# TensorE's attention steps gathered between feed-forward runs in a fused decoder layer

## The chip, the cores and the metric

The kernel runs on one core of one Trainium2 chip. The metric is the device time of one execution in microseconds (us), as the median of several; lower is better.

## The reference, cut to what matters

One decoder layer over x of 32 sequences, 128 tokens each, width 256, all float32:

```
x = x + linear_attention(layernorm(x))          # 16 heads of 16, phi = elu + 1, causal running sums, q/k/v/o projections
x = x + cross_attention(layernorm(x), ctx)      # 16 heads of 16, softmax(q k / 4) v, no output projection
x = x + ffn(layernorm(x))                       # ternary weights with one scale per output:
      h = silu(s1 * (x w1)) * (s2 * (x w2))     # 256 -> 1024, "gate"
      h = gelu(h1s * (h h1)); h = gelu(h2s * (h h2))   # 1024 -> 1024 twice, "hidden"
      y = w3s * (h w3)                          # 1024 -> 256, "w3"
```

## The kernel before, in words

**Tiles.** The 32 sequences are worked through in 16 groups g of two sequences (256 tokens) for the two attentions, and in 8 turns f of four sequences (512 tokens) for the feed-forward. Turn f takes groups 2f and 2f+1, and runs while the attention of later groups runs beside it. Products that need float32 accuracy are made of parts: a value is split in a rounded and a rest part, and the matmuls of the parts are summed in PSUM.

**Steps and due times.** The order of every engine's work is written out by a planner at build time. Each step (a name, a group or turn, and an index n) is put with `put` on one or more engines, with a due time in nominal us: for attention `begin(g) + stretch * t`, for the feed-forward `FF0 + TURN * f + t`. Sorted by due time, these lists are the program of each engine: SyncE (`sync`) issues the DMAs, GpSimd (`gpsimd`), ScalarE (`scalar`), VectorE (`vector`) and TensorE (`tensor`) compute. Engines run their list in order, and wait at each step on semaphores. The due times only sort; they are not enforced, and in the trace most steps run some 15 to 30 us later than their nominal time.

**TensorE's steps.** The feed-forward steps are `gate`, `hidden` and `w3`, of four matmuls of 512 columns each (lines 982, 997, 1012). The attention steps are projections (`q`, `k`, `xk`, `xq`, line 825; `v`, `xv`, line 835; `project`, line 937: 12 or 6 matmuls of 256 columns), transposes (`ln1T`, `ln2T`, `x2T`, `xn3T`, line 814; `lin_turn`, `x_turn`, line 860; `o_turn`, line 928; `shift`, line 955), and the "quarter" steps, which use the array by quarters: scores (`lin_scores`, `max`, `x_scores`, lines 871 and 878) and sums (`lin_sums`, `x_sums`, line 851). After sorting, a loop over TensorE's list moves quarter steps: where two of them have only feed-forward steps between them and their due times differ by less than JOIN (1.44), the earlier is moved behind those feed-forward steps, to stand next to the later.

**Banks.** After that a second pass gives each TensorE step the PSUM banks that come free first by the due times of the steps that read them. A step waits, before it writes a bank, for the reader of the bank's last content. So `max` n=1 of a group, which needs four banks, waits for four readers (for example VectorE's `q` of the next group, or `max_of`).

**The other engines' steps named below.** On VectorE: `gated` (lines 776, 779) multiplies gates, `max_of` (line 745) takes maxima out of the `max` banks, `q` (lines 653, 658) forms phi(q), `lin_turn` (lines 666 to 673) divides, `lin_mask` (line 728) masks, `o_turn` (line 647) makes a rest part, `ln1_stats` (lines 637 to 640) and `ln1` (line 643) belong to the first layernorm, and `low_bits` (lines 794, 796) checks a piece of the weights, 48 times in all, each piece loaded before by SyncE's `load_bits` (line 432) into one buffer. `load_bits` waits until the `low_bits` before it is done. SyncE's `ring` (line 423) loads a weight chunk into one of four slots when TensorE has used up the slot's last content.

Of the kernel before, what the change touches and what calls it, by code (L numbers as in the profile page):

```python
# [5 lines left out]
def decoder_layer_program(nc, x, ctxT, wqT, wkT, wvT, woT, bv, bo, xqT, xkT, xvT,  # L6
# [37 lines left out]
    def put(start, step, g, n=0, stretch=1.0, **slots):  # L44
        for engine, t in slots.items():
            engines[engine].append((start + stretch * t, step, g, n))

    for g in range(G):
        at, stretch = begin(g)
        early = g < len(EARLY)  # L50

        def steady(step, n=0, **slots):
            put(at, step, g, n, stretch, **slots)

        steady("load_x", sync=-26.63)
# [6 lines left out]
        steady("v", tensor=-3.78, vector=-0.18)
        steady("load_xb", sync=1.22)
        steady("bias", gpsimd=9.03)
        steady("load_ctx", sync=-1.48)
        steady("ctx", scalar=9.15, gpsimd=8.15)
        for b in range(GB):
            steady("lin_scores", b, tensor=-0.89 + 4.6 * b)
        for n in range(NU):
            u = 0.34 + 1.09 * n  # L70
            steady("lin_mask", n, vector=u + 0.02)
        for b in range(GB):
            for h in range(2):
                if early:
                    u = 2.15 + 5.15 * b + 2.64 * h
                else:
                    u = 4.18 + 7.14 * b + 0.02 * h
                steady("lin_sums", 2 * b + h, tensor=u - 0.32)
            steady("lin_out", b, scalar=u + 1.21)
            u = 7.2 + 4.71 * b  # L80
            steady("lin_turn", b, tensor=u - 0.39, vector=u + 0.5)
            steady("o_turn", b, tensor=u + 0.93, scalar=u + 3.59, vector=u + 2.25)
            steady("project", b, tensor=u + 3.88, vector=u + 5.03, gpsimd=u + 6.25)
            steady("ln2", b, vector=u + 6.35)
        steady("ln2T", tensor=17.76, scalar=17.95, vector=18.63)
        steady("xq", tensor=21.95, scalar=22.34)
        steady("xk", tensor=16.76, scalar=20.6)
        steady("xv", tensor=11.7, scalar=16.21)
        for b in range(GB):
            steady("max", b, tensor=23.23 + 2 * b)  # L90
            steady("x_scores", b, tensor=29.28 + 3 * b)
        for n in range(NU):
            b, u = n // 4, n % 4
            steady("max_of", n, vector=24.37 + .72 * n)
            w = 30.6 + 3.45 * b + 0.09 * u
            steady("x_exp", n, scalar=w + 0.1)
        for b in range(GB):
            for h in range(2):
                if early:
                    u = 31.71 + 3.3 * b + 0.45 * h  # L100
                else:
                    u = 31.3 + 3.72 * b + 0.01 * h
# [22 lines left out]
    def out_of_window(t):  # L125

        for first, last in stretches:
            if first < t < last:
                return last
        return t  # L130

    for f in range(NF):
        at = FF0 + TURN * f
        for p in range(2):
            put(at, "xn3T", 2 * f + p, tensor=-10.49 + 2.6 * p, scalar=-5.65 + 2.6 * p, vector=-5.32 + 2.6 * p)
            put(at, "x2T", 2 * f + p, tensor=11 + 1.5 * p, scalar=12.78 + 1.5 * p)
        put(at, "keep_xn", f, sync=16.34)
        put(at, "keep_x2", f, sync=14.37)
        for m in range(KH):
            u = 2 * QUARTER * m  # L140
            for z in range(2):
                put(at, "gate", f, 2 * m + z, tensor=u + QUARTER * z)
            put(at, "tanh", f, m, scalar=u + QUARTER + 0.93)
            put(at, "gated", f, m, vector=u + 2 * QUARTER + 0.64)
            put(at, "gate_round", f, m, scalar=u + 2 * QUARTER + 4.43)
            put(at, "gate_rest", f, m, gpsimd=u + 2 * QUARTER + 5.72)
        for n in range(2 * KH):
            for q in range(4):
                k = 4 * n + q
                if n % KH < 2:  # L150
                    k = 8 * (n // 2) + (6 + n % 2 if q == 3 else 3 * (n % 2) + q)
                put(at, "hidden", f, 4 * n + q, tensor=QUARTER * (2 * KH + k))
            u = QUARTER * (2 * KH + 4 * (n + 1) + (n % KH == 0) * 3) + .5
            put(at, "gelu", f, n, scalar=out_of_window(at + u) - at)
            put(at, "gelu_rest", f, n, vector=out_of_window(at + u) - at + 1.6)
        for c in range(C):
            for q in range(4):
                k = 6 + c if q == 3 else 3 * c + q
                put(at, "w3", f, 4 * c + q, tensor=QUARTER * (10 * KH + k))
            put(at, "out", f, c, vector=TURN + .4 + c, sync=TURN + 1.6 + c)  # L160
        for j in range(NCH):
            if f == 0 and j < RING:
                u = -44.53 + j
            elif j < RING:
                u = (-7.74, -1, -6, 1.8)[j]
# [46 lines left out]
    with outer:  # L212
# [7 lines left out]
        ctx = ExitStack()  # L220
        with ctx:
            def sb(name, shape, dt=F32):
                return ctx.enter_context(nc.sbuf_tensor(name, shape, dt))
# [26 lines left out]
            v, xv = sb("v", [P, GB, H, 2 * HD]), sb("xv", [P, GB, H, 2 * HD])  # L250
# [19 lines left out]
            ring = sb("weight_ring", [P, RING, KH * P], F32R)  # L270
# [72 lines left out]
            while pending:  # L343
                t, step, g, n = pending.pop()
# [681 lines left out]
        ctx = ExitStack()  # L1026
        with ctx:
# [7 lines left out]
            gate = sb("general_gate", [P, FT])  # L1035
# [233 lines left out]
```

How the kernel before makes its waits and increments, by code:

```python
            def wait_freed(eng, step, g, n):  # L367
                _, s, count = release(step, g, n)
                eng.wait_ge(s, count)
# [8 lines left out]
            def wait_count(eng, s, count):  # L378
                if count > 0:
                    eng.wait_ge(s, count)
# [5 lines left out]
            def wait_full(eng, f, tile):  # L387
                f, tile = (f, tile - NFULL) if tile >= NFULL else (f - 1, tile - NFULL + 3 * KH)
                if f >= 0:
                    if tile < KH:
                        eng.wait_ge(gate_lo, KH * f + tile + 1)
                    else:
                        eng.wait_ge(h_lo, 2 * KH * f + tile - KH + 1)
# [14 lines left out]
                def load_ring(f, j):  # L408
                    if j >= RING:
                        used = j - RING
                        if used < 4:
                            eng.wait_ge(gate_psum, 2 * KH * f + 4 * used + 4)
                        else:
                            eng.wait_ge(h_psum, 2 * KH * f + used - 3)
                    elif f > 0:
                        if j % 2 == 0:
                            eng.wait_ge(w3_half, C * (f - 1) + j // 2 + 1)
                        else:
                            eng.wait_ge(o_psum, C * (f - 1) + j // 2 + 1)
                    if f == 0:
                        eng.wait_ge(w_copied[j // RING % 2], 16 * RING * (j // RING // 2 + 1))
                    n = WSRC[j].shape[1]
                    eng.dma_start(ring[:, j % RING, 0:n].bitcast(F32), w_d[j, :, 0:n]).then_inc(ring_loaded[j % RING], 16)
```

## Time and profile before

| | us |
|---|---|
| three runs: median (lowest, highest) | 1128.82 (1127.39, 1129.23) |
| the profiled execution: its own time | 1130.69 |
| its span | 1128.9 |
| TensorE matmul busy | 1087.5 |
| VectorE busy | 694.1 |
| ScalarE busy | 541.8 |
| GpSimd busy | 196.0 |

The profile is of one execution. Busy times are sums over an engine's instructions. PE is TensorE (its records of consecutive matmuls overlap, so distances are read here from start to start), DVE is VectorE, ACT is ScalarE, POOL is GpSimd, SPq is SyncE's DMA queue.

### The profile page before, as it was taken

What the parts mean: (1) busy time and instruction counts of PE and PEld (TensorE: products, weight loads), DVE (VectorE), ACT (ScalarE), POOL (GpSimd) and SP (SyncE); (2) the same over time, 40 slices, a digit from 0 to 9 for tenths busy, and PEclk for the clock granted to TensorE, in tenths of its full rate; (3) what the DMA queues carried; (4) which work ended last, traced back from release to release, by engine and by line L of the source; (5) the groups of instructions that cost most, each with busy time, mean ns of one, the idle gap of its engine ahead of it and who ended that gap; (6) DMA issues with size and microseconds to landing.
All of it is one profiled execution on the core that took longest, in us unless ns stands there. A gap on an engine that the chain in (4) does not pass through costs nothing.

```text
span 1128.9 us, 25213 instructions
## 1 busy us (share of the span) xinstructions
PE 1087.5 (96%) x10114; PEld 900.6 (80%) x10114; DVE 694.1 (61%) x1580; ACT 541.8 (48%) x909; POOL 196.0 (17%) x266
## 2 busy tenths in 40 slices
PE   4878999999999999999999999999999999999997
PEld 4767878888888888888888888888788888878886
DVE  5678764558656676567656686466765667534521
ACT  3244644536446454645546364373544645354532
POOL 1122320013201132022210222002320023100300
PEclk8899999999999999999999999999999999999999
DMA  3243554344323444324533354233433344434742
GB/s 117 66 163 110 185 186 144 122 138 162 129 92 114 135 160 131 104 85 145 188 113 104 99 172 137 94 123 126 163 104 109 110 150 141 132 108 131 242 154 76
DMA packets 62502, 148.62 MB, mean 132 GB/s; under 512 B 5936, under 2 KB 21424, under 8 KB 62384
## 3 DMA queue, kind: packets, MB, share of 16 engines
q1 hardware_dynamic: 58928, 135.44, 36.6%
q10 hardware_dynamic: 3456, 11.54, 3.2%
q8 instruction: 83, 1.36, 0.5%
q14 instruction: 35, 0.29, 0.1%
HBM read 130.17 MB, written 28.31 MB: 140 GB/s over the span
## 4 chain that ended last, share of the span: by engine, by line
PE 93%; DVE 3%; issue 1%; ACT 1%; DMA 1%; ACTq 0%; POOL 0%; SPq 0%; DVEq 0%; POOLq 0%
PE bank L997 42%; PE bank L982 10%; PE bank L878 9%; PE bank L825 8%; PE bank L851 5%; PE bank L1012 5%; PE bank L835 4%; PE bank L860 3%; PE bank L814 2%; PE bank L937 2%; PE bank L871 1%; PE bank L928 1%; PE bank L955 1%; DVE att_l L728 0%; DMA weight_ring<-weights_scratch 0%
## 5 line engine op out<-in xcount | busy, mean ns | idle before, releaser
L997 PE MATMUL bank<-hidden_b,weight_ring 128*128 128x512 f32 x1024 | 257.5, 398 | 0.3
L997 PE MATMUL bank<-hidden_a,weight_ring 128*128 128x512 f32 x1024 | 256.1, 397 | 0.0
L997 PEld LDWEIGHTS bank<-hidden_a,weight_ring 128*128 128x128 f32 x1024 | 185.7, 188 | 38.8 <-issue 3.4
L997 PEld LDWEIGHTS bank<-hidden_b,weight_ring 128*128 128x128 f32 x1024 | 184.9, 188 | 39.6 <-issue 3.8
L625 ACT ACTIVATE hidden_full<-bank,columns_sb 128x512 f32<-128x512 f32 x128 | 88.2, 689 | 232.9 <-PE bank L997 232.7
L982 PE MATMUL bank<-hidden_b,weight_ring 128*128 128x512 f32 x512 | 132.3, 399 | 0.5 <-DVE ex L658 0.3
L511 POOL TENSOR_TENSOR hidden_a<-hidden_full,hidden_a 128x512 fp32r<-128x512 f32 x64 | 82.3, 1289 | 194.0 <-ACT hidden_a L620 194.0
L728 DVE TENSOR_TENSOR att_l<-bank,cst 128x512 f32<-128x512 f32 x128 | 85.5, 684 | 39.7 <-PE bank L878 34.9
L982 PEld LDWEIGHTS bank<-hidden_b,weight_ring 128*128 128x128 f32 x512 | 92.2, 189 | 18.2 <-DMA weight_ring<-weights_scratch 0.7
L485 POOL TENSOR_TENSOR ve<-mv,eps 128x1 f32<-128x1 f32 (+1 forms) x80 | 19.7, 247 | 487.7 <-DVE mv L640 487.7
L784 DVE TENSOR_TENSOR hidden_a<-hidden_full,hidden_a 128x512 fp32r<-128x512 f32 x64 | 44.2, 691 | 79.0 <-ACT hidden_a L631 78.9
L745 DVE TENSOR_REDUCE mx<-bank 128x4 f32<-128x512 f32 x128 | 82.6, 682 | 9.2 <-PE bank L878 9.1
L784 DVE TENSOR_TENSOR hidden_b<-hidden_full,hidden_b 128x512 fp32r<-128x512 f32 x64 | 43.9, 686 | 67.4 <-ACT hidden_b L631 67.3
L595 ACT ACTIVATE att_x<-bank 128x512 f32<-128x512 f32 x128 | 66.1, 603 | 37.7 <-PE bank L878 37.6
L1012 PE MATMUL bank<-hidden_a,weight_ring 128*128 128x512 f32 x256 | 67.0, 399 | 0.0
L530 ACT ACTIVATE sums<-bank 128x512 f32<-128x512 f32 x64 | 38.5, 602 | 52.5 <-PE bank L851 52.5
L615 ACT ACTIVATE hidden_full<-bank,s1h 128x512 f32<-128x512 f32 x64 | 44.0, 688 | 35.8 <-PE bank L982 35.4
L776 DVE SCALAR_TENSOR_TENSOR hidden_full<-hidden_full,bank 128x512 f32<-128x512 f32 x64 | 43.7, 683 | 28.3 <-ACT hidden_full L615 28.1
L1012 PEld LDWEIGHTS bank<-hidden_a,weight_ring 128*128 128x128 f32 x256 | 45.8, 188 | 8.0
L500 POOL TENSOR_TENSOR ctxs<-ctx_in,ctxs 128x512 fp32r<-128x512 f32 x16 | 21.0, 1313 | 175.9 <-ACT ctxs L545 175.9
L488 POOL TENSOR_TENSOR rstd<-ve,mhalf 128x1 f32<-128x1 f32 (+1 forms) x80 | 50.0, 625 | 6.3
L779 DVE SCALAR_TENSOR_TENSOR hidden_full<-bank,s,hidden_full 128x512 f32<-128x512 f32 x64 | 48.1, 751 | 4.5 <-PE bank L982 2.4
(119 smaller groups left out, 1659.8 us busy)
## 6 DMA issues: line engine op xcount, KB each, us to landing
weight_ring<-weights_scratch SPq DMA_DIRECT2D x160, 512.0 KB, 3.4
weights_scratch<-in_h ACTq DMA_DIRECT2D x16, 512.0 KB, 4.7
xn3T_scratch<-hidden_b SPq DMA_DIRECT2D x16, 512.0 KB, 6.0
weight_ring<-weights_scratch SPq DMA_DIRECT2D x32, 256.0 KB, 2.7
weight_bits<-in_h SPq DMA_DIRECT2D x32, 256.0 KB, 3.8
x_in<-in_x SPq DMA_DIRECT2D x16, 256.0 KB, 3.6
xb<-in_x SPq DMA_DIRECT2D x16, 256.0 KB, 4.5
ctx_in<-in_ctxT SPq DMA_DIRECT2D x16, 256.0 KB, 4.3
```

The lines of the kernel that those rows point to most:

```text
L511: eng.tensor_tensor(HA[:, 1, n, :], full[:, n % NFULL, :], HA[:, 0, n, :].bitcast(F32), ALU.subtract)\
L595: eng.activation(att_x[:, (NU * g + n) % NX, :, :], pbank("x_scores", g, n)[:, :].rearrange("p (j s) -> p j s", j=4), ACT.Exp, scale=SCALE ...
L625: eng.activation(full[:, (KH + n) % NFULL, :], pbank("hidden", g, n)[:, :], ACT.Gelu, scale=sc).then_inc(h_full, 1)
L728: eng.tensor_tensor(att_l[:, (NU * g + n) % NL, :, :], pbank("lin_scores", g, n)[:, :].rearrange("p (j s) -> p j s", j=4), causal.rearrang ...
L745: eng.tensor_reduce(mx[:, b, 4 * r:4 * r + 4], pbank("max", g, n)[:, :].rearrange("p (j t) -> p j t", j=4), AX.X, ALU.max).then_inc(max_do ...
L784: eng.tensor_tensor(dst[:, 1, m, :], full[:, (KH + n) % NFULL, :], dst[:, 0, m, :].bitcast(F32), ALU.subtract)\
L825: mm = eng.matmul(pbank(step, g)[:, m * T:(m + 1) * T], w[:, i, c, m * P:(m + 1) * P], src[:, j, c, :], start=(c + i + j == 0), stop=(c == ...
L851: mm = eng.matmul(pbank(step, g, b)[32 * j:32 * j + 32, u * S:(u + 1) * S], vt[:, b, 8 * m + 2 * (n % 4) + e, :], att[:, (NU * g + n) % sl ...
L878: mm = eng.matmul(pbank(step, g, 4 * b + r)[:, j * S:(j + 1) * S], stationary(rows, e, m, b), moving(rows, e, m, b), start=not shifted, st ...
L982: mm = eng.matmul(pbank(step, g, n)[:, :], ring[:, n // 4, at_:at_ + P], HB[:, part, kk, :], start=(kk == 0 and part == 0), stop=(kk == C ...
L997: mm = eng.matmul(pbank(step, g, n)[:, :], ring[:, slot, kk * P:(kk + 1) * P], src[:, part, kk, :], start=(kk == 0 and part == 0), stop=(k ...
L1012: mm = eng.matmul(pbank(step, g, c)[:, :], ring[:, slot, kk % 4 * P:(kk % 4 + 1) * P], HA[:, part, kk, :], start=(kk == 0 and part == 0), ...
```

## The change

GATHER = 1 is new. The loop that moves TensorE's steps now looks at every step that is not feed-forward. Two such steps with only feed-forward steps between them are put side by side when their due times differ by less than JOIN (both quarter steps) or less than GATHER (all other pairs). With it most due times are written anew, of all engines. Nothing that is computed changes.

```diff
+    GATHER = 1
@@ attention, due times (a selection)
-        steady("load_x", sync=-26.63)
-        steady("ln1_stats", vector=-17.81, gpsimd=-16.41)
-        steady("ln1", vector=-13.07)
+        steady("load_x", sync=-25.57)
+        steady("ln1_stats", vector=-18.45, gpsimd=-15.85)
+        steady("ln1", vector=-11.62)
-        steady("q", tensor=-7.66, scalar=-6.73, vector=-5.37)
+        steady("q", tensor=-7.67, scalar=-6.7, vector=-5)
-            steady("lin_out", b, scalar=u + 1.21)
+            steady("lin_out", b, scalar=u + 1.36)
-        steady("xk", tensor=16.76, scalar=20.6)
-        steady("xv", tensor=11.7, scalar=16.21)
+        steady("xk", tensor=16, scalar=21.24)
+        steady("xv", tensor=12.01, scalar=15.67)
...
@@ feed-forward, SyncE and the weight check
-            put(at, "xn3T", 2 * f + p, tensor=-10.49 + 2.6 * p, scalar=-5.65 + 2.6 * p, vector=-5.32 + 2.6 * p)
+            put(at, "xn3T", 2 * f + p, tensor=-10.67 + 2.6 * p, scalar=-5.69 + 2.6 * p, vector=-5.46 + 2.6 * p)
-            put(at, "ring", f, j, sync=u - 4.82)
+            put(at, "ring", f, j, sync=u - 4.32)
-            u = 185.23 + 117.17 * i + 18.33 * j
-            put(0, "load_bits", i, j, sync=u - 4.56)
-            put(0, "low_bits", i, j, vector=u + 11.29)
+            u = 185.23 + 116.9 * i + 18.33 * j
+            put(0, "load_bits", i, j, sync=u - 12.42)
+            put(0, "low_bits", i, j, vector=u + 11.2)
...
@@ the loop over TensorE's list
     order = program["tensor"]
+    feed_forward = ("gate", "hidden", "w3")
+    quarters = ("lin_scores", "max", "x_scores", "lin_sums", "x_sums")
     for i in reversed(range(len(order))):
-        if order[i][1] in ("lin_scores", "max", "x_scores", "lin_sums", "x_sums"):
+        if order[i][1] not in feed_forward:
             j = i - 1
-            while j > 0 and order[j][1] in ("gate", "hidden", "w3"):
+            while j > 0 and order[j][1] in feed_forward:
                 j -= 1
-            if j >= 0 and order[j][1] in ("lin_scores", "max", "x_scores", "lin_sums", "x_sums") and order[i][0] - order[j][0] < JOIN:
+            both = order[i][1] in quarters and order[j][1] in quarters
+            if 0 <= j < i - 1 and order[j][1] not in feed_forward and order[i][0] - order[j][0] < (JOIN if both else GATHER):
                 order.insert(i - 1, (order[i][0], *order.pop(j)[1:]))
```

## Rows read from the trace of the kernel before

**Rows 1.** The page: busy us by engine, and the ending chain by engine.

```profile
PE 1087.5 (96%) x10114; PEld 900.6 (80%) x10114; DVE 694.1 (61%) x1580; ACT 541.8 (48%) x909; POOL 196.0 (17%) x266
PE 93%; DVE 3%; issue 1%; ACT 1%; DMA 1%; ACTq 0%; POOL 0%; SPq 0%; DVEq 0%; POOLq 0%
```

**Rows 2.** Busy us by stretch: length, engines (instructions), granted clock, DMA share, GB/s.

```profile
50.00:100.00 50.00, 37.82 (x680) 31.33 (x680) 38.02 (x104) 19.96 (x39) 8.09 (x16) 0.97 0.42 131
...
200.00:300.00 100.00, 99.83 (x990) 82.32 (x989) 66.72 (x149) 51.12 (x87) 21.21 (x26) 1.00 0.45 146
```

**Rows 3.** TensorE in order of time, group 10: start us, us, [wait].

```profile
657.70 1.17 PE L878 MATMUL bank<-xkz,xqf 32*128 32x128 f32 x32
...
674.22 0.40 PE L871 MATMUL bank<-shiftT,onesb 2*128 2x512 bf16 x4
```

**Rows 4.** TensorE, the same steps of group 12.

```profile
792.06 1.17 PE L878 MATMUL bank<-xkz,xqf 32*128 32x128 f32 x32
...
801.04 1.17 PE L878 MATMUL bank<-xkz,xqf 32*128 32x128 f32 x32 [1.68 <-DVE qf L658]
...
811.59 0.39 PE L871 MATMUL bank<-shiftT,onesb 2*128 2x512 bf16 x4
```

**Rows 5.** One microsecond of that stretch, columns as in Rows 2.

```profile
803.00:804.00 1.00, 1.00 (x7) 1.00 (x6) 0.97 (x4) 0.00 (x0) 0.00 (x0) 0.50 0.07 16
```

**Rows 6.** VectorE in order of time, group 12.

```profile
796.48 0.69 DVE L776 SCALAR_TENSOR_TENSOR hidden_full<-hidden_full,bank 128x512 f32<-128x512 f32 x1 [1.76 <-ACT hidden_full L615]
...
797.87 0.42 DVE L794 TENSOR_SCALAR weight_bits<-weight_bits 128x512 int32<-128x512 int32 x1
...
798.93 0.95 DVE L653 TENSOR_SCALAR ex<-ex 128x512 f32<-128x512 f32 x1
...
800.70 1.28 DVE L745 TENSOR_REDUCE mx<-bank 128x4 f32<-128x512 f32 x2
```

**Rows 7.** TensorE: feed-forward matmuls in a row, then beside a transpose step, then a projection.

```profile
314.82 3.34 PE L997 MATMUL bank<-hidden_a,weight_ring 128*128 128x512 f32 x14
318.00 0.60 PE L814 MATMUL bank<-cst,x_in 128*128 128x128 f32 x4
...
662.46 1.17 PE L982 MATMUL bank<-hidden_b,weight_ring 128*128 128x512 f32 x4
663.46 0.60 PE L814 MATMUL bank<-cst,x 128*128 128x128 f32 x4
663.82 1.17 PE L982 MATMUL bank<-hidden_b,weight_ring 128*128 128x512 f32 x4
...
241.63 1.07 PE L1012 MATMUL bank<-hidden_a,weight_ring 128*128 128x512 f32 x4
242.54 1.58 PE L825 MATMUL bank<-ctxs,xwk 128*128 128x256 f32 x12
243.96 1.08 PE L1012 MATMUL bank<-hidden_a,weight_ring 128*128 128x512 f32 x4
```

**Rows 8.** VectorE, ScalarE and TensorE in order of time, 102 to 106 us.

```profile
102.21 0.17 DVE L666 TENSOR_SCALAR denom<-bank 128x16 f32<-128x16 f32 x1
...
103.65 0.42 DVE L637 BATCH_NORM_STATS2 stats<-x_in 128x6 f32<-128x256 f32 x1
...
104.73 0.39 DVE L647 TENSOR_TENSOR oT<-bank,oT 128x256 fp32r<-128x256 f32 x1
...
103.66 0.38 ACT L574 ACTIVATE oT<-bank 128x256 fp32r<-128x256 f32 x1 [1.19 <-PE bank L928]
...
103.19 0.44 PE L928 MATMUL bank<-cst,o 128*128 128x128 f32 x2
...
105.18 0.98 PE L937 MATMUL bank<-wo,oT 128*128 128x256 f32 x6 [0.75 <-DVE oT L647]
```

**Rows 9.** SyncE: its waits (us in total, times, longest); issues with us to landing.

```profile
SPq L432 <- DVE low_bits L796: 6.1, 4, 2.1
...
weight_ring<-weights_scratch SPq DMA_DIRECT2D x32, 256.0 KB, 2.7
```

More of the change, by code:

```diff
@@ L53, in steady @@
             put(at, step, g, n, stretch, **slots)
-        steady("load_x", sync=-26.63)
-        steady("ln1_stats", vector=-17.81, gpsimd=-16.41)
-        steady("ln1", vector=-13.07)
-        steady("ln1T", tensor=-9.6, scalar=-9.01, vector=-8.43)
-        steady("q", tensor=-7.66, scalar=-6.73, vector=-5.37)
-        steady("k", tensor=-5.1, scalar=-4.61, vector=-3.1)
-        steady("k_heads", vector=-2.9)
[L62 to L66, printed above, removed]
+        steady("load_x", sync=-25.57)
+        steady("ln1_stats", vector=-18.45, gpsimd=-15.85)
+        steady("ln1", vector=-11.62)
+        steady("ln1T", tensor=-9.64, scalar=-9.01, vector=-8.43)
+        steady("q", tensor=-7.67, scalar=-6.7, vector=-5)
+        steady("k", tensor=-5.24, scalar=-4.61, vector=-3.1)
+        steady("k_heads", vector=-2.9)
+        steady("v", tensor=-3.82, vector=-0.18)
+        steady("load_xb", sync=1.17)
+        steady("bias", gpsimd=9.6)
+        steady("load_ctx", sync=-2.52)
+        steady("ctx", scalar=9.15, gpsimd=8.82)
         for b in range(GB):
-            steady("lin_scores", b, tensor=-0.89 + 4.6 * b)
+            steady("lin_scores", b, tensor=-0.93 + 4.6 * b)
         for n in range(NU):
-            u = 0.34 + 1.09 * n
+            u = 0.35 + 1.09 * n
             steady("lin_mask", n, vector=u + 0.02)
@@ L74, in decoder_layer_program @@
                 if early:
-                    u = 2.15 + 5.15 * b + 2.64 * h
+                    u = 2.15 + 5.38 * b + 2.64 * h
                 else:
                     u = 4.18 + 7.14 * b + 0.02 * h
-                steady("lin_sums", 2 * b + h, tensor=u - 0.32)
-            steady("lin_out", b, scalar=u + 1.21)
+                steady("lin_sums", 2 * b + h, tensor=u - 0.36)
+            steady("lin_out", b, scalar=u + 1.36)
             u = 7.2 + 4.71 * b
-            steady("lin_turn", b, tensor=u - 0.39, vector=u + 0.5)
-            steady("o_turn", b, tensor=u + 0.93, scalar=u + 3.59, vector=u + 2.25)
-            steady("project", b, tensor=u + 3.88, vector=u + 5.03, gpsimd=u + 6.25)
+            steady("lin_turn", b, tensor=u - 0.43, vector=u + 0.5)
+            steady("o_turn", b, tensor=u + 0.89, scalar=u + 3.59, vector=u + 2.13)
+            steady("project", b, tensor=u + 3.84, vector=u + 5.03, gpsimd=u + 6.39)
             steady("ln2", b, vector=u + 6.35)
-        steady("ln2T", tensor=17.76, scalar=17.95, vector=18.63)
-        steady("xq", tensor=21.95, scalar=22.34)
-        steady("xk", tensor=16.76, scalar=20.6)
-        steady("xv", tensor=11.7, scalar=16.21)
+        steady("ln2T", tensor=17.72, scalar=17.95, vector=18.35)
+        steady("xq", tensor=21.91, scalar=22.34)
+        steady("xk", tensor=16, scalar=21.24)
+        steady("xv", tensor=12.01, scalar=15.67)
         for b in range(GB):
-            steady("max", b, tensor=23.23 + 2 * b)
-            steady("x_scores", b, tensor=29.28 + 3 * b)
+            steady("max", b, tensor=23.3 + 2 * b)
+            steady("x_scores", b, tensor=29.24 + 3 * b)
         for n in range(NU):
@@ L134, in decoder_layer_program @@
         for p in range(2):
-            put(at, "xn3T", 2 * f + p, tensor=-10.49 + 2.6 * p, scalar=-5.65 + 2.6 * p, vector=-5.32 + 2.6 * p)
-            put(at, "x2T", 2 * f + p, tensor=11 + 1.5 * p, scalar=12.78 + 1.5 * p)
-        put(at, "keep_xn", f, sync=16.34)
-        put(at, "keep_x2", f, sync=14.37)
+            put(at, "xn3T", 2 * f + p, tensor=-10.67 + 2.6 * p, scalar=-5.69 + 2.6 * p, vector=-5.46 + 2.6 * p)
+            put(at, "x2T", 2 * f + p, tensor=11.58 + 1.5 * p, scalar=12.75 + 1.5 * p)
+        put(at, "keep_xn", f, sync=21.99)
+        put(at, "keep_x2", f, sync=13.19)
         for m in range(KH):
@@ L142, in decoder_layer_program @@
                 put(at, "gate", f, 2 * m + z, tensor=u + QUARTER * z)
-            put(at, "tanh", f, m, scalar=u + QUARTER + 0.93)
+            put(at, "tanh", f, m, scalar=u + QUARTER + 0.86)
             put(at, "gated", f, m, vector=u + 2 * QUARTER + 0.64)
-            put(at, "gate_round", f, m, scalar=u + 2 * QUARTER + 4.43)
-            put(at, "gate_rest", f, m, gpsimd=u + 2 * QUARTER + 5.72)
+            put(at, "gate_round", f, m, scalar=u + 2 * QUARTER + 4.66)
+            put(at, "gate_rest", f, m, gpsimd=u + 2 * QUARTER + 3.33)
         for n in range(2 * KH):
@@ L162, in decoder_layer_program @@
             if f == 0 and j < RING:
-                u = -44.53 + j
+                u = -44.42 + j
             elif j < RING:
-                u = (-7.74, -1, -6, 1.8)[j]
+                u = (-11.57, -0.79, -6, 1.58)[j]
             elif j < 2 * RING:
```

10 lines of the change are left out of this document (5 added, 5 removed).

## The prediction

> **What bounds the kernel now.** I read the page first. Matmuls fill 96% of the span and the chain that ends last is TensorE's for 93% [rows 1]. The busy times by stretch split the kernel in two. From about 110 us on TensorE is full: 99.83 of 100 us in one stretch, at a granted clock of 1.00. Before that, from 50 to 100 us, it works 37.82 of 50, since the first groups' attention is a chain from engine to engine and no feed-forward stands beside it yet [rows 2]. So there are three places where the change can act: what it costs TensorE to go between kinds of step, the few waits left in the full part, and the early chain.
>
> The timeline of TensorE shows one wait in the full part that is worth more than all the others. The same steps, from `max` n=0 to `x_scores` n=0, take 674.22 - 657.70 = 16.52 us in group 10 [rows 3] and 811.59 - 792.06 = 19.53 in group 12 [rows 4]. The 3.01 us between them are a wait of 1.68 us of `max` n=1 for VectorE's `q` [rows 4], and some 1.3 us of half clock behind it: the granted clock is 0.50 at 803 us [rows 5], that is 1.2 instead of 2.4 GHz, after TensorE had stood idle for the wait. VectorE shows why. It idles 1.76 us before `gated` at 796.48, then works `gated`, a `low_bits` (797.87 to 798.93, 1.06 us) and only then `q`, which frees the bank [rows 6].
>
> **What the diff does to the orders.** I worked out the sort, the loop and the bank pass by the planner's own rules, once with the old and once with the new due times. The result is smaller than the title. TensorE's list of 1248 steps has 281 feed-forward runs before and 262 after, so 19 visits to attention fall away; 55 positions differ. In groups 4, 6, ..., 14 the order `xn3T`, 4 matmuls, `project`, 4 matmuls, `xk` becomes `xn3T`, `project`, `xk` (two visits less, twelve in all); in groups 5, 7, ..., 15 `project` and `xk` meet (one less, six in all); one more falls away earlier. Many steps stay where they are although their due times are new: the loop and the new due times act on nearly the same places. GpSimd's list does not change. ScalarE's changes only up to 145 us.
>
> **Visits.** Fourteen feed-forward matmuls in a row take 318.00 - 314.82 = 3.18 us, 0.227 each, so four take 0.908 [rows 7]. Beside a projection four take 0.91, and the projection's twelve take 1.42: a visit costs no more than 0.02. Beside a transpose step the four take 1.00 and the four transposes 0.36, together 1.36 [rows 7]. Nothing in these rows says what four transposes take among their like; if it is the 0.44 that TensorE's records of two show, such a visit costs about 0.02 as well. So 19 x 0.02 = 0.4 us gained, with bounds of 0 (the cost only moves into the neighbour) and 19 x 0.09 = 1.7 (the whole 0.09 by which the four matmuls beside a transpose are longer). I take 0.4, since 13 or more of the visits are projections. `xk` runs one feed-forward step (0.9 us) earlier; its input is ready long before, and nobody waits for its output sooner.
>
> **The wait of group 12.** In the new VectorE order `low_bits` 5,0 stands between two `max_of` of group 12, ahead of `gated`. There it falls into the idle 1.76 us [rows 6] and costs nothing (1.06 < 1.76). Also `max_of` n=2 now comes before `q`, and by the new bank pass `max` n=1 waits for `max_of` n=2 and no longer for `q`. One `max_of` is 0.64 us (1.28 for two), `q` was 800.70 - 798.93 = 1.77. What is late next: VectorE itself. From `gated` to the last `max_of` it has no idle time in group 10, and `x_scores` starts when it is through. So the swap of `q` and `max_of` brings the other even groups nothing (their short wait moves to `x_scores`), but group 12 falls back to the 16.52 us of group 10: 3.0 us gained, against this profiled execution. No other `low_bits` of the new order falls into that stretch of an even group. The bounds: 1.7 us if the half clock does not come with the wait in the timed runs, 3.0 if it does, 0 if the wait comes back elsewhere.
>
> **The early chain.** `ln1_stats` of group 3 moves ahead of VectorE's `lin_turn` 2,0. It takes 104.73 - 103.65 = 1.08 us [rows 8]. So `lin_turn` and TensorE's `o_turn` (103.19) come 1.08 later. ScalarE's copy ended 104.04 and will end about 105.1; VectorE's rest part, which stood in the queue until 104.73, can start at 105.1 instead, and TensorE's `project`, which waits for it at 105.18 [rows 8], starts 0.4 us later. Behind it comes the full part, which can't take this back: 0.4 lost, bounded by 0 and 1.08. ScalarE's `lin_out` 1,1 moves behind three of `x_exp`, which are ready before it; I put that at 0 to 0.3 lost. `ln1` of groups 1 and 3 goes behind steps that TensorE waits for, and VectorE's `gated` 0,4 goes ahead of `q` 3: 0 to 0.4 gained. Together 0.3 lost.
>
> **SyncE.** `load_bits` is now due 18.33 - 12.42 = 5.9 after the u of the piece before, and the `low_bits` that it waits for at 11.2: 5.3 us too early, where before it was due 13.8 against 11.29. In the trace it waited four times, 2.1 us at most [rows 9]; now it will wait most times, up to 5 us and more, and the `ring` loads, `load_x`, `load_xb` and `load_ctx` queued behind it wait with it. A ring slot is refilled three chunks ahead of its use, 12 quarters of 1.557 = 18.7 nominal us; less 5.3, it has 13 for a landing. The last chunk of `w3` has least: six quarters, 9.3 - 5.3 = 4.0, against 2.7 to landing [rows 9]. It just holds. Cost 0; if the cover is gone, about 1 us in one turn.
>
> **The sum.** Against the profiled execution: 1130.69 - 0.4 - 3.0 + 0.3 = 1127.6. That execution is 1.87 above the median of the runs. The likeliest reason is that the half clock of group 12 (1.3 us) does not come in each run. Against the median the gain is then 0.4 + 1.7 - 0.3 = 1.8, up to 3.1 if the median holds the half clock too: 1127.0 to 1125.7. I take a gain of 2.2, so 1126.6.
>
> **Rivals.**
> *The wait was no part of the time.* The timed runs scatter over 1.8 us; if `q` is mostly early enough there, or if a wait of the same kind arises elsewhere from the 831 changed bank places, only the visits and the early loss are left: 1128.82 - 0.1, say 1128.5. For it speaks that the wait is in one group of six; against it that it follows from an order that is the same in each run.
> *All of it and more.* The half clock is in each run of before, and the early chain loses nothing: 1128.82 - 0.4 - 3.0 = 1125.4.
> *The early chain decides, and it is slower.* TensorE idles a quarter of the time there [rows 2], so every delay there is passed on. If `lin_turn`'s 1.08 is passed on whole, `lin_out`'s 0.3 with it, the last `w3` chunk is late by 1 and group 12 gives only 1.7: 1128.82 + 2.4 - 2.1 = 1129.1; slower only if group 12 gives nothing, 1131.2.
> *The clock, and it is much slower.* Each loss of the clock costs 1.3 us, as group 12 shows [rows 4, 5]. If attention steps standing together were little enough work to lower the clock, the twelve turns of groups 4 to 15 would cost 15.6: 1142. From two such losses on the gain is gone. Against it: transposes and projections side by side already stand in the full part, at 1.00 over 100 us [rows 2].
> The Trainium skill speaks for this last rival (TensorE: Matmul & The Clock Gate, Part 4: PE-mode transpose): the clock gate does not count transposes as busy the way it counts other matmuls. The rows show no fall of the clock at a transpose, only one after a wait.
>
> **Chances.** The forecast, 1125.7 to 1127.9, has 0.55; no gain 0.20; all and more 0.14; the early chain 0.07; the clock 0.04. A change under 0.2% (2.26 us) can hardly be told from none here. Faster by more means below 1126.56: about half of the forecast and all of the third case, 0.42. Slower by more is the clock and part of the early chain, 0.08; within, 0.50. The range, 1124.8 to 1129.3, takes in the first three cases and most of the fourth.
>
> **What would show it.** Right: group 12's 19.53 us fall to about 16.5, no granted clock of 0.5 near 803 us, 38 fewer changes between feed-forward and other rows of TensorE, `project` 2,0 about 0.4 us later than at 105.18, more and longer waits of SyncE's line 432 without one of TensorE's for `weight_ring`. Wrong: a new TensorE wait over 1 us after 110 us, or 16.5 us in group 12 and yet no less time, which would put the loss into the early chain.

## The result, and the profile after

The changed kernel is slower. Seven runs of each, on one chip:

| | before | after |
|---|---|---|
| median us (lowest to highest) | 1129.23 (1127.39 to 1131.46) | 1136.46 (1134.03 to 1137.07) |
| ratio of the times, 95% interval | 1 | 1.0055 [1.0041, 1.0069] |
| profiled execution: own time | 1130.69 | 1135.28 |
| its span | 1128.9 | 1133.5 |

The ratio is 6.2 us (4.6 to 7.8); the two profiled executions lie 4.6 apart. The page of the changed kernel, busy us by engine and the chain that ended last:

```profile
PE 1084.7 (96%) x10114; PEld 896.8 (79%) x10114; DVE 701.4 (62%) x1580; ACT 542.9 (48%) x909; POOL 195.9 (17%) x266
PE 86%; DVE 9%; issue 3%; ACT 1%; DMA 0%; ACTq 0%; POOL 0%; SPq 0%; DVEq 0%; POOLq 0%
```

Against [rows 1], the number of instructions of each engine is the same, and yet VectorE is busy for 7.3 us more, with 9% of the chain in place of 3%. Nothing was added to it, so some of its instructions must take longer. The windows of the changed kernel:

```profile
50.00:100.00 50.00, 38.29 (x697) 31.42 (x697) 38.17 (x105) 19.96 (x39) 8.02 (x16) 0.97 0.42 133
200.00:300.00 100.00, 98.47 (x979) 81.05 (x978) 67.03 (x147) 50.59 (x86) 20.82 (x26) 1.00 0.45 140
803.00:804.00 1.00, 1.00 (x8) 0.91 (x7) 1.00 (x3) 0.75 (x2) 0.56 (x1) 1.00 0.91 266
```

TensorE has lost 1.4 us in the 100 us from 200 on, where it was full [rows 2]; at 803 us the clock is 1.00, where it was 0.50 [rows 5]. TensorE's waits from 110 us on (line, releaser: us in total, times, longest), of the changed kernel and then of the kernel before:

```profile
PE bank L876 <- DVE mx L750: 5.9, 6, 1.2
PE bank L830 <- DVE qf L663: 2.1, 6, 0.4
PE bank L1026 <- DVE low_bits L804: 1.0, 1, 1.0
PE bank L883 <- DVE mx L750: 0.6, 1, 0.6
```

```profile
PE bank L878 <- DVE qf L658: 1.7, 1, 1.7
PE bank L1021 <- DVE low_bits L799: 1.0, 1, 1.0
PE bank L982 <- DVE ex L658: 0.3, 1, 0.3
PE bank L928 <- DVE o L673: 0.3, 1, 0.3
PE bank L982 <- DMA weight_ring<-weights_scratch: 0.2, 1, 0.2
```

(A line of the changed kernel has a number 5 higher than before.) The one wait for `q` is gone, as forecast, and two new kinds came, six times each: once in each even group from 4 to 14. They are 8.0 us together, and both are for VectorE. (The single wait of 0.6 us stands in the early part, at 126 us.) The same steps in groups 10 and 12 of the changed kernel, to be held against [rows 3] and [rows 4]:

```profile
661.58 1.17 PE L883 MATMUL bank<-xkz,xqf 32*128 32x128 f32 x32
...
679.49 0.40 PE L876 MATMUL bank<-shiftT,onesb 2*128 2x512 bf16 x4 [0.88 <-DVE mx L750]
...
797.19 1.17 PE L883 MATMUL bank<-xkz,xqf 32*128 32x128 f32 x32
...
815.10 0.40 PE L876 MATMUL bank<-shiftT,onesb 2*128 2x512 bf16 x4 [0.88 <-DVE mx L750]
```

From `max` n=0 to `x_scores` n=0 it is 17.91 us in both. Group 12 gained 1.62 (19.53 before), and each of the other five even groups lost 1.39 (16.52 before; group 6 lost 1.44): 4 x 1.39 + 1.44 - 1.62 = 5.4 us lost.

**Where the 1.39 us are.** VectorE in order of time, first of the kernel before and then of the changed one, group 10:

```profile
662.11 0.69 DVE L776 SCALAR_TENSOR_TENSOR hidden_full<-hidden_full,bank 128x512 f32<-128x512 f32 x1 [1.76 <-ACT hidden_full L615]
...
663.50 0.42 DVE L653 TENSOR_SCALAR ex<-ex 128x512 f32<-128x512 f32 x1
663.96 0.88 DVE L658 SCALAR_TENSOR_TENSOR qf<-bank,bq,ex 128x256 f32<-128x256 f32 x2
...
668.86 0.42 DVE L653 TENSOR_SCALAR ex<-ex 128x512 f32<-128x512 f32 x1
...
671.48 1.39 DVE L713 TENSOR_SCALAR kz<-ex,cst 128x512 f32<-128x512 f32 x2
672.80 1.27 DVE L745 TENSOR_REDUCE mx<-bank 128x4 f32<-128x512 f32 x2
```

```profile
665.99 0.69 DVE L781 SCALAR_TENSOR_TENSOR hidden_full<-hidden_full,bank 128x512 f32<-128x512 f32 x1 [1.72 <-ACT hidden_full L620]
...
667.38 0.68 DVE L750 TENSOR_REDUCE mx<-bank 128x4 f32<-128x512 f32 x1
667.98 1.42 DVE L658 TENSOR_SCALAR ex<-ex 128x512 f32<-128x512 f32 x1
...
673.73 1.33 DVE L658 TENSOR_SCALAR ex<-ex 128x512 f32<-128x512 f32 x1
...
677.27 0.87 DVE L718 TENSOR_SCALAR kz<-ex,cst 128x512 f32<-128x512 f32 x2
678.06 1.28 DVE L750 TENSOR_REDUCE mx<-bank 128x4 f32<-128x512 f32 x2
```

The clip in phi(q) (`ex = min(ex, 1)`, 128x512) took 0.42 us and takes 1.42; that in phi(k) took 0.42 and takes 1.33; `k_heads` took 1.39 for its two instructions and takes 0.87. That is 1.00 + 0.91 - 0.52 = 1.39, all of the loss. GpSimd beside it, before and after:

```profile
663.93 1.29 POOL L511 TENSOR_TENSOR hidden_a<-hidden_full,hidden_a 128x512 fp32r<-128x512 f32 x1 [4.26 <-ACT hidden_a L620]
669.31 1.30 POOL L511 TENSOR_TENSOR hidden_a<-hidden_full,hidden_a 128x512 fp32r<-128x512 f32 x1 [4.08 <-ACT hidden_a L620]
```

```profile
667.82 1.29 POOL L516 TENSOR_TENSOR hidden_a<-hidden_full,hidden_a 128x512 fp32r<-128x512 f32 x1 [4.23 <-ACT hidden_a L625]
...
673.49 1.29 POOL L516 TENSOR_TENSOR hidden_a<-hidden_full,hidden_a 128x512 fp32r<-128x512 f32 x1 [4.37 <-ACT hidden_a L625]
```

Before, each clip begins first and has just ended when GpSimd's `gate_rest` (1.29 us) starts: 663.50 + 0.42 = 663.92 against 663.93, and 668.86 + 0.42 = 669.28 against 669.31. It is not the clip that `gate_rest` waits for: it starts 0.08 us behind the end of ScalarE's `gate_round` in both kernels (663.86 before, 667.74 after). After, `max_of` n=2 stands ahead of the clip, `gate_rest` begins first (667.82 against 667.98, 673.49 against 673.73), and the clip ends only 0.29 and 0.28 us behind it. The clip reads and writes SBUF alone. The product rows of `q` behind it in the kernel before (0.88 for two, one input in PSUM) run beside `gate_rest`, and are no longer for it (each of the 32 takes 0.47 to 0.49 us, 11 of them beside it). The group of clips over the whole execution, before and after (us in total, mean ns | idle before them):

```profile
L653 DVE TENSOR_SCALAR ex<-ex 128x512 f32<-128x512 f32 x32 | 14.9, 466 | 23.1 <-ACT ex L556 13.7 <-ACT ex L550 9.3
```

```profile
L658 DVE TENSOR_SCALAR ex<-ex 128x512 f32<-128x512 f32 x32 | 25.4, 792 | 19.6 <-ACT ex L561 13.2 <-ACT ex L555 6.3
```

The clips are busy for 10.5 us more, and `k_heads` for 3.4 less (17.4 to 14.0): 7.1 of VectorE's 7.3.

So the theory, called P below: the two engines hold each other off for one whole instruction, and the new order makes GpSimd first. The Trainium skill states this rule (SBUF — State Buffer, Who interferes with whom): a VectorE tensor_scalar can enter a mode in which it needs the port pair that GpSimd uses too, and "Whoever issues first gets the shared pair for the whole instruction". The rows agree: GpSimd's instruction comes first and keeps its 1.29 us, and the clip is 1.00 and 0.91 us longer. A sharing of the port in which only VectorE loses could give such rows as well; x9 tells the two apart.

### The profile page after: what moved, and what is told of

It is laid out like the page before. It is cut to its first block, busy times and chain, and to the rows that moved or that the text cites. A ratio compares the mean times of both kernels' runs of the same rounds, so it can differ in the third digit from the quotient of the medians.

```text
span 1133.5 us, 25213 instructions
## 1 busy us (share of the span) xinstructions
PE 1084.7 (96%) x10114; PEld 896.8 (79%) x10114; DVE 701.4 (62%) x1580; ACT 542.9 (48%) x909; POOL 195.9 (17%) x266
## 4 chain that ended last, share of the span: by engine, by line
PE 86%; DVE 9%; issue 3%; ACT 1%; DMA 0%; ACTq 0%; POOL 0%; SPq 0%; DVEq 0%; POOLq 0%
PE bank L1002 42%; PE bank L883 8%; PE bank L830 7%; PE bank L987 7%; PE bank L1017 5%; PE bank L856 5%; PE bank L840 3%; DVE mx L750 3%; PE bank L865 3%; PE bank L942 2%; PE bank L819 2%; DVE ex L658 1%; DVE hidden_full L781 1%; PE bank L876 1%; DVE att_l L733 1%
## 5 line engine op out<-in xcount | busy, mean ns | idle before, releaser
L1002 PE MATMUL bank<-hidden_a,weight_ring 128*128 128x512 f32 x1024 | 254.7, 397 | 0.0
L1017 PE MATMUL bank<-hidden_a,weight_ring 128*128 128x512 f32 x256 | 64.7, 397 | 0.0
```

The costliest lines, as they stand in the source:

```text
L1002: mm = eng.matmul(pbank(step, g, n)[:, :], ring[:, slot, kk * P:(kk + 1) * P], src[:, part, kk, :], start=(kk == 0 and part == 0), stop=(k ...
L1017: mm = eng.matmul(pbank(step, g, c)[:, :], ring[:, slot, kk % 4 * P:(kk % 4 + 1) * P], HA[:, part, kk, :], start=(kk == 0 and part == 0), ...
```

## The experiments

Each ratio is to runs of the kernel before on the same chip (medians 1129.2 to 1130.6). The columns of this table are medians (n), the ratio to before with its 95% interval, us from `max` n=0 to `x_scores` n=0 in groups 4 / 12, and the mean of the 32 clips in ns. The last two are from one profiled execution of each kernel.

| kernel | us (n) | ratio | 4 / 12 | clip |
|---|---|---|---|---|
| before | 1129.23 (7) | 1 | 16.52 / 19.53 | 466 |
| after | 1136.46 (7) | 1.0055 [1.0041, 1.0069] | 17.91 / 17.91 | 792 |
| x1 after, `q` first | 1129.01 (10) | 0.9994 [0.9984, 1.0004] | 16.53 / 16.52 | 447 |
| x2 before, `q` late | 1135.91 (5) | 1.0047 [1.0025, 1.0068] | 17.93 / 17.98 | 777 |
| x3 after, short `gate_rest` | 1125.93 (8) | 0.9972 [0.9961, 0.9983] | 16.24 / 16.24 | 434 |
| x4 before, new loop | 1129.38 (10) | 0.9995 [0.9984, 1.0005] | 16.53 / 18.11 | 489 |
| x5 before, new due times of the bits | 1127.86 (11) | 0.9984 [0.9975, 0.9993] | 16.52 / 16.51 | 448 |
| x6 x4 + x5 + `k_heads` | 1127.27 (11) | 0.9978 [0.9969, 0.9986] | 16.37 / 16.37 | 472 |
| x7 x1 + `k_heads` | 1128.34 (12) | 0.9986 [0.9974, 0.9998] | 16.36 / 16.36 | 447 |
| x8 after, old loop | 1137.31 (4) | 1.0073 [1.0057, 1.0089] | 17.90 / 17.90 | 789 |
| x9 after, `gate_rest` in halves | 1130.46 (12) | 1.0004 [0.9989, 1.0019] | 16.94 / 16.94 | 613 |
| x10 x6 with halves | 1126.45 (9) | 0.9965 [0.9953, 0.9978] | 16.37 / 16.36 | 438 |

**x1, the changed kernel with `q` ahead of `max_of` again.**

```diff
-        steady("q", tensor=-7.67, scalar=-6.7, vector=-5)
+        steady("q", tensor=-7.67, scalar=-6.7, vector=-5.37)
```

> The changed kernel with one due time put back: VectorE's q at -5.37, so that q stands ahead of max_of n=2 again from group 4 on. Theory P (VectorE's clipping of q, one fast instruction with input and output in SBUF, and GpSimd's gate_rest hold each other up, and the new order starts q just after gate_rest instead of just before): the clip of q and of k falls from 1.42 and 1.33 us to 0.43 each in the even turns, x_scores n=0 of groups 4 to 14 comes about 1.3 us earlier in each, and the time falls by some 8 us, to 1127 to 1129. Rival Q (the queue: one more max_of ahead of q, or the new banks, delays something by itself): the clips stay long or only 0.7 us per even group comes back, 1132 or more. Rival G (the gathered TensorE order is what costs): no change, 1136.

Measured 1129.01: one due time of 0.37 gives back the whole loss. Its clip and `gate_rest` of group 10:

```profile
667.51 0.42 DVE L658 TENSOR_SCALAR ex<-ex 128x512 f32<-128x512 f32 x1
```

```profile
667.93 1.29 POOL L516 TENSOR_TENSOR hidden_a<-hidden_full,hidden_a 128x512 fp32r<-128x512 f32 x1 [4.25 <-ACT hidden_a L625]
```

The clip begins 0.42 us before `gate_rest` and takes 0.42. The order is the cause; that the meeting with GpSimd is what it works through is not yet shown. Of the gain that was forecast for the rest of the change, only 0.7 us can be seen (from 1.8 less than before to 0.5 more), though group 12 has lost its wait here.

**x2, the kernel before with that one due time of the changed one.**

```diff
-        steady("q", tensor=-7.66, scalar=-6.73, vector=-5.37)
+        steady("q", tensor=-7.66, scalar=-6.73, vector=-5)
```

> The kernel before with one due time of the change: VectorE's q at -5, which puts max_of n=2 ahead of q from group 4 on and leaves TensorE's order as it was. Theory P: the clips of q and k become 1.42 and 1.33 us in six groups, and the time rises by 7 to 9 us, to 1137. Rival Q with a queue cost alone: 0.7 us in each of six groups, 1133. Rival G: no change, 1129.

Measured 1135.91, 1.0047: 5.3 us lost (2.8 to 7.7), less than the 7 to 9 expected. The expectation counted six groups; group 12 falls from 19.53 to 17.98 here, so that the six stretches together lose 5.5. The same number put into the kernel before does nearly all of the change's harm, with the same 17.9 us and long clips (1.41 and 1.37 us in group 10). So the loss needs nothing else from the diff: not the loop, not the other due times, not SyncE. The pass that gives out the banks reads this due time too; x3 and x9 keep the changed kernel's banks and take the loss away all the same.

**x3, the changed kernel with a short `gate_rest`.**

```diff
-                        eng.tensor_tensor(HA[:, 1, n, :], full[:, n % NFULL, :], HA[:, 0, n, :].bitcast(F32), ALU.subtract)\
+                        wd = FT if g == 0 else 32
+                        eng.tensor_tensor(HA[:, 1, n, 0:wd], full[:, n % NFULL, 0:wd], HA[:, 0, n, 0:wd].bitcast(F32), ALU.subtract)\
```

> The changed kernel with GpSimd's gate_rest cut to 32 of its 512 columns from the second feed-forward turn on (the rest parts of the gate are left as they were for the other columns, so the output differs). Order, waits and banks are those of the changed kernel. Theory P: with GpSimd at work for some 0.1 us instead of 1.29, the clips of q and k take 0.43 us, or at most 0.2 more, and the time falls by 8 us or a little more, to 1126 to 1129. Rivals Q and G: the order alone sets the time, 1135 to 1137, and the clip of q keeps its 1.42.

Measured 1125.93 with the order of the changed kernel; the other 480 columns of the gate's rest parts are not computed. `gate_rest` and the clip of `q` in group 10:

```profile
663.12 0.25 POOL L517 TENSOR_TENSOR hidden_a<-hidden_full,hidden_a 128x32 fp32r<-128x32 f32 x1 [5.40 <-ACT hidden_a L626]
```

```profile
663.28 0.42 DVE L659 TENSOR_SCALAR ex<-ex 128x512 f32<-128x512 f32 x1
```

The clip comes 0.16 us behind `gate_rest` as in the changed kernel, and takes 0.42. `q` is as late in VectorE's list as there, and the stretch takes 16.24 us. That GpSimd's instruction is what the clip waits for is thereby shown. It also tells what all such meetings cost: 0.28 us a group in the kernel before as well (16.52 - 16.24), where `k_heads` is the row that is visibly long (1.39 for its two instructions). TensorE has no idle time in these 16.24 us (0.19 before), so a VectorE with still less to do could not shorten them.

**x4, the kernel before with the new loop.**

```diff
+    GATHER = 1
...
+            both = order[i][1] in quarters and order[j][1] in quarters
+            if 0 <= j < i - 1 and order[j][1] not in feed_forward and order[i][0] - order[j][0] < (JOIN if both else GATHER):
```

> The kernel before with the new loop (GATHER = 1) and all its old due times: TensorE's gathering alone, 274 feed-forward runs instead of 281. By the cost of a visit (0.02 us) it saves 0.1 us: 1129, no change. Rival G (gathered attention steps themselves cost, by later VectorE and ScalarE input or a lower clock): 1133 or more. If a quarter step or transpose is moved over the narrow place of VectorE and GpSimd, theory P allows a loss too, and the clip of q or k would show it.

Measured 1129.38, no difference, with 274 feed-forward runs in place of 281. The parts of the profile don't say "nothing" but cancel: from the first `gate` to the first `hidden` it takes 33.52 us, 1.9 more than before's 31.62, and from there to the last feed-forward matmul 979.22, 2.7 less than 981.94. The early loss is two waits of TensorE that the kernel before has not:

```profile
PE bank L882 <- DVE mx L749: 1.0, 1, 1.0
PE bank L986 <- DVE qf L662: 0.8, 1, 0.8
```

The second is behind a new meeting: a clip of `q` at 126.67 us takes 1.19, as the expectation had allowed. Of the gain, 1.4 us are group 12's, and they are not the loop's. `max` n=1 waits there as long as before, but no half clock follows:

```profile
801.98 1.17 PE L882 MATMUL bank<-xkz,xqf 32*128 32x128 f32 x32 [1.67 <-DVE qf L662]
```

```profile
780.00:820.00 40.00, 38.24 (x380) 1.00 0.53 172
```

So the half clock does not follow this wait in each execution. That gathering alone makes the kernel slower by what the change lost is refuted; that it costs nothing at any place is not shown.

**x5, the kernel before with the new due times of the weight check.** The stall of group 12 came from a `low_bits`.

```diff
-            u = 185.23 + 117.17 * i + 18.33 * j
-            put(0, "load_bits", i, j, sync=u - 4.56)
-            put(0, "low_bits", i, j, vector=u + 11.29)
+            u = 185.23 + 116.9 * i + 18.33 * j
+            put(0, "load_bits", i, j, sync=u - 12.42)
+            put(0, "low_bits", i, j, vector=u + 11.2)
```

> The kernel before with the changed due times of load_bits and low_bits alone (u with 116.9, -12.42 and +11.2). low_bits 5,0 then stands between two max_of of group 12, ahead of gated. Theory P counts the stall of group 12 (3.0 us in the profile of before) as one of VectorE's queue and not of the port: max n=0 to x_scores n=0 of group 12 falls from 19.53 to 16.5 us, and SyncE's blocked ring loads cost nothing. If that stall is in the timed runs of before too, the time is 1126 to 1127.8; rival N (it is an accident of the profiled execution): 1129 to 1130, and the profile shows the 16.5 us all the same.

Measured 1127.86, 0.9984: 1.8 us gained (0.8 to 2.8) in the timed runs, and group 12 at 16.51. The profiled execution does not show the gain in its time (1130.55, the highest of the eleven). It lost it again in one place, a ring chunk that came late. TensorE's wait from 1000 to 1060 us, and the window:

```profile
PE bank L982 <- DMA weight_ring<-weights_scratch: 1.8, 1, 1.8
```

```profile
1030.00:1045.00 15.00, 13.16 (x60) 0.98 0.73 235
1045.00:1055.00 10.00, 10.00 (x44) 0.86 0.37 106
```

Beside it before had 14.76 of 15 us and 1.00 in both. A wait of 1.8 us was followed by some lost clock, 3.2 us in all: x5 is 3.32 us ahead of before at the same matmul before the wait (1029.38 against 1032.70) and 0.12 ahead behind it (1056.78 against 1056.90). SyncE shows why a chunk can be late: it now waits at `load_bits` for `low_bits`, with the ring loads behind it (x6 and x10, with the same due times, have one such wait of TensorE too, of 1.0 and 0.6 us):

```profile
SPq L432 <- DVE low_bits L796: 151.0, 38, 11.0
```

**x6, x4 and x5 together, and `k_heads` 0.5 later from group 4 on.**

```diff
-        steady("k_heads", vector=-2.9)
+        steady("k_heads", vector=-2.9 if early else -2.4)
```

> x5 with the new loop (GATHER = 1) and with k_heads moved one place later on VectorE from group 4 on, behind max_of n=6 (due -2.4 instead of -2.9). In the kernel before, the first half of k_heads takes 1.00 us instead of 0.48 in six groups, beside GpSimd's gate_rest. If the port is held by whoever comes first, k_heads starts after gate_rest has ended and takes 0.48 twice; max n=0 to x_scores n=0 falls to 16.0 us in groups 4 to 14: 3.0 us for the stall of group 12 and 6 x 0.5 for k_heads: 1123.5 to 1125. If the narrow place shifts to another pair (the clip of k, or gate_rest 5), the gain of k_heads is lost: 1126 to 1127.

Measured 1127.27, 0.9978; expected 1123.5 to 1125. `k_heads` falls to 480 ns in the mean (584 before), as expected, but the stretch gives only 0.15 us a group (16.37), not 0.5. In size the expectation failed, and x3 tells why: TensorE's own work takes 16.24 of the 16.52 us, so 0.28 is the most that a stretch can give. In group 10 VectorE's last `max_of` now ends 0.52 us ahead of `x_scores` (0.15 before), and TensorE idles 0.08. Again the early part takes 33.56 us, as in x4, with the same two waits.

**x7, x1 with the same shift of `k_heads`** (the diffs of x1 and x6).

> The changed kernel with VectorE's q at -5.37 (as in the run with q put back) and k_heads behind max_of n=6 from group 4 on. Theory P: 3 us under the kernel with q alone put back, 1125 to 1126.5, with k_heads at 0.48 and the stretch of the even groups at 16.0 us. If only the order of the port matters and the even groups' stretch is bound elsewhere: no change to it, 1128 to 1129.

Measured 1128.34, 0.9986; expected by P 1125 to 1126.5 and 16.0 us in the stretch. Each of the six even groups gains 0.11 to 0.17 us, as in x6 and for the same reason. The time can't be told from x1's (0.9994) by the intervals.

**x8, the changed kernel with the old loop** (x4's diff, backwards).

> The changed kernel with the loop of before: 276 feed-forward runs instead of 262, all new due times. By the cost of a visit (0.02 us) it is 0.3 us slower than the changed kernel, 1136 to 1137: the loss stays, since it comes from VectorE's order. Rival G (the gathering costs): back to 1129 to 1131.

Measured 1137.31, 1.0073, with 276 feed-forward runs in place of 262. The loss stays, as expected. From the first `hidden` to the last feed-forward matmul it takes 987.61 us against 986.27: without 14 visits the changed kernel is 1.3 us faster there, in one profile of each. The ratios of the timed runs (1.0073 and 1.0055) agree in sign, but their intervals overlap.

**x9, the changed kernel with each `gate_rest` in two halves.** P says that a clip waits for one instruction. A sharing of the port by columns says that it waits as long in either form.

```diff
+                        eng.tensor_tensor(HA[:, 1, n, 0:FT // 2], full[:, n % NFULL, 0:FT // 2], HA[:, 0, n, 0:FT // 2].bitcast(F32), ALU.subtract)
+                        eng.tensor_tensor(HA[:, 1, n, FT // 2:FT], full[:, n % NFULL, FT // 2:FT], HA[:, 0, n, FT // 2:FT].bitcast(F32), ALU.subtract)\
```

> The changed kernel, each `gate_rest` of GpSimd written as two instructions of 256 columns in place of one of 512; the result is the same. Theory P (whoever issues first holds the other engine off for one whole instruction): `q`'s clip, which starts 0.16 us after `gate_rest`, waits only for the first half (some 0.65 us) and takes about 0.9 in place of 1.42; `k`'s clip 0.85 in place of 1.33; the stretch from `max` n=0 to `x_scores` n=0 of groups 4 to 14 takes 16.9 us in place of 17.91, 6 us less in all: about 1130.5. Rival S (the two engines share the port column by column, so that the same number of columns in flight costs the same): clips stay at 1.3 to 1.4, 17.9 us, 1136.5. Rival L (GpSimd keeps the hold from one instruction to its next): the same as S in the time, with the clip's end behind the second half's end; in S it is before it.

Measured 1130.46; expected 1130.5 by P, 1136.5 by both rivals. VectorE's clips of `q` and `k` in group 10, and GpSimd's halves:

```profile
664.31 0.86 DVE L659 TENSOR_SCALAR ex<-ex 128x512 f32<-128x512 f32 x1
...
669.50 0.91 DVE L659 TENSOR_SCALAR ex<-ex 128x512 f32<-128x512 f32 x1
```

```profile
664.15 0.74 POOL L516 TENSOR_TENSOR hidden_a<-hidden_full,hidden_a 128x256 fp32r<-128x256 f32 x1 [3.94 <-ACT hidden_a L626]
664.84 0.92 POOL L517 TENSOR_TENSOR hidden_a<-hidden_full,hidden_a 128x256 fp32r<-128x256 f32 x1
...
669.40 0.74 POOL L516 TENSOR_TENSOR hidden_a<-hidden_full,hidden_a 128x256 fp32r<-128x256 f32 x1 [3.64 <-ACT hidden_a L626]
670.10 0.92 POOL L517 TENSOR_TENSOR hidden_a<-hidden_full,hidden_a 128x256 fp32r<-128x256 f32 x1
```

The clip gets in between the halves: it ends at 665.17, 0.28 us behind the first half (664.15 + 0.74), and the second half only at 665.76. The second, which has the clip ahead of it, is 0.18 longer than the first. So it is with all 12 clips that meet a first half; of the other second halves all but two take 0.72 to 0.75, and those two stand behind the first instruction of a `low_bits`. The engines take turns by instruction. Rivals S and L are refuted.

The kernel before had two such meetings of a clip too, one in the early part (132.33 us, 1.24 long) and one at the clip of [rows 6]. GpSimd's row beside the latter:

```profile
798.30 1.29 POOL L511 TENSOR_TENSOR hidden_a<-hidden_full,hidden_a 128x512 fp32r<-128x512 f32 x1 [4.26 <-ACT hidden_a L620]
```

It ends at 799.59, and the clip at 798.93 + 0.95 = 799.88, 0.29 us behind.

**x10, x6 with the halves.**

> The kernel before with the new loop, the new due times of `load_bits` and `low_bits` and `k_heads` 0.5 later (the best kernel so far, 0.9978 of before, 16.37 us in the stretch), and each `gate_rest` written as two instructions of 256 columns. Theory P: what is left of collisions there, 0.1 to 0.2 us in a group of the steady part and those of the early part, is at most halved: 1126.7, 0.9973; the second instruction's own overhead on GpSimd is hidden, since GpSimd is busy for 17 per cent. Rival O (the halves' overhead reaches ScalarE and TensorE through the buffers that `gate_rest` frees): 1128 or more, with new waits behind GpSimd.

Measured 1126.45, 0.9965 [0.9953, 0.9978]: the fastest of all, 4.0 us (2.5 to 5.3) below before. Its stretches are those of x6, so the halves gained nothing there that can be seen. In the early part they did in the profile: the clips at 126.7 and 134 us, 1.19 and 1.23 long in x6, take 0.65 and 0.68, and the part from the first `gate` to the first `hidden` 32.68 in place of 33.56. By the timed runs, whose intervals overlap, x6 and x10 may be one kernel.

## Why the prediction was wrong

**The step that failed** is "So the swap of `q` and `max_of` brings the other even groups nothing". It took VectorE's durations as fixed, whatever the order, and put the cost of the swap at nothing. The swap itself was found, and so was the reason why it must matter: the prediction says that from `gated` to the last `max_of` VectorE has no idle time, and `x_scores` starts when it is through. In such a stretch a longer instruction is passed on whole. What was not asked is what runs on GpSimd beside each instruction that moves. The swap puts the clip 0.6 us later (one `max_of`), `gate_rest` becomes first, and two clips cost 1.00 and 0.91 us, less 0.52 that `k_heads` no longer waits: +1.39 in five groups, and in group 12 the same taken from its gain of 3.01. x1 and x2 show it from both sides, x3 and x9 show the mechanism. The prediction's own sign of being wrong came: the wait for `max_of` is 1.18 us long in group 6.

No rival held it either. The slow ones were placed in the early chain, SyncE and the clock. (The 1131.2 of the early chain's worst case leaves out the 0.4 of the visits, which its 1129.1 has; 1130.8 by the prediction's own terms.) The sign could have been read from the trace of before: the clip has mean 466 ns where it took 0.42 us alone, the row at 798.93 shows 0.95 for the same clip [rows 6], 0.63 us into a `gate_rest`, and `k_heads` one of its two instructions at about 1.0. Rows of one form with two durations were the sign, and [rows 6] stood in the argument with 0.95 taken as the clip's cost.

**Group 12**: right in its cause and in what is late next but for the clips. 16.52 us come in x1, and x5 has 16.51 from `low_bits` alone, so there the bits' due times do it and the swap isn't needed. In the timed runs x5 is worth 1.8 us (0.8 to 2.8), with what SyncE's waits cost in it; the prediction had 1.7 to 3.0. Its reason for the lower bound is borne out by x4: the same wait, 1.67 us, and no half clock.

**Visits**: 0.4 was neither borne out nor refuted. x8 against the changed kernel gives 1.3 us for 14 of them. x1 has all 19 fewer; from the first `hidden` to the last feed-forward matmul it takes 978.78 us, 3.16 less than before, and its stretches account for 2.8 of them, which leaves 0.3. Both are within the bounds of 0 and 1.7, each from single profiles.

**The early part**: the 0.4 us at `project` 2,0 came, though as a time of its own it shows nothing: it starts at 104.80, 0.38 earlier than before, since executions of one order differ by more than that ahead of it (last section). Counted from the same step of group 2's sums shortly before (100.16 before, 99.42 after), it starts 5.38 us on in place of 5.02, 0.36 later, and the first `gate` 0.36 later too. What the prediction did not have is 0.40 more behind it, from the first `gate` to the first `hidden` (32.02 against 31.62), with the wait of 0.6 for `max_of` in it.

**SyncE**: cost 0 in the changed kernel's profile (no wait of TensorE for `weight_ring`, though line 437 waits 41 times, 10.4 us at most). The warning "about 1 us in one turn" fits x6 and x10 (1.0 and 0.6) and was too small for x5, whose profile shows 1.8 of wait and 3.2 in all.

**The clock rival**: nothing of it. TensorE's granted clock is 1.00 over 200 to 300 us, at 803 us, and in the mean from 100 to 1120 us, with projections and transposes side by side. The rule of the Trainium skill named there (TensorE: Matmul & The Clock Gate, Part 4: PE-mode transpose) costs nothing that these rows show.

**The sum with what was measured**, profile to profile: -0.4 (up to the first `gate`) + 0.4 (from there to the first `hidden`) + 5.4 (the stretches: clips, less group 12) - 1.1 (all else up to the last feed-forward matmul, the visits in it; a remainder, 986.27 - 981.94 - 5.4) + 0.3 (behind it) = 4.6 us, as 1135.28 - 1130.69. The medians differ by 7.2 and their ratio by 6.2 (4.6 to 7.8); the profiled execution of after lies 1.2 under its median and that of before 1.5 over its own, which is within the scatter of single executions.

## What to carry to other kernels

Where a planner swaps two VectorE steps in a stretch without idle time, look at what GpSimd runs beside each at the new place: here a clip (tensor_scalar, SBUF to SBUF) that came 0.2 us behind a GpSimd instruction waited for all that was left of it, and one that came 0.4 us ahead lost nothing. Search the trace of before for rows of one form with two durations, and hold them against GpSimd's rows; here each such clip and `k_heads` was a meeting, and told its price. Where the order can't be changed, shorter instructions on GpSimd help: halving `gate_rest` took 5.8 us back (1.0055 against 1.0004) without touching the order.

## What the runs showed of the hardware

- The clip of 128x512 takes 0.42 us alone, and 1.42, 1.33 and 0.95 when GpSimd's 1.29 us subtraction has begun 0.16, 0.24 and 0.63 us before it. Its end is then 0.28 to 0.29 us behind the end of the GpSimd instruction, of the whole one as of a half: so in all 94 long clips and `k_heads` instructions of the twelve profiles. GpSimd's 1.29 us are the same with and without a clip behind it. `tensor_reduce` from a bank was not longer beside it (0.68 to 0.69 us in the changed kernel, 33 of 128 beside it), nor were the products that read a bank (0.47 to 0.49).
- The margin is small: before, the clips of `q` and `k` in group 10 ended 0.01 and 0.03 us before `gate_rest` started.
- TensorE's granted clock fell to 0.50 behind an idle time of 1.68 us in the profile of before [rows 4, 5], and stayed at 1.00 behind one of 1.67 at the same step in x4's.
- The early clock varies between executions of one order. In x1, whose order up to the first `gate` is the changed kernel's, the granted clock from 50 to 100 us was 0.86 against 0.97, and the first `gate` started at 111.52 us against 108.01. Where two kernels are compared by one profile each, 3.5 us can be this.

```profile
50.00:100.00 50.00, 39.70 (x640) 32.69 (x644) 35.44 (x97) 20.09 (x39) 7.29 (x14) 0.86 0.37 118
```
